# Scans over both halves of a state, and four of sixteen products with B moved to ScalarE

## The reference

```python
u, z = split(x @ Win.T)                       # 2 x 256 channels
u = silu(causal_conv4(u) + convb)
dtr, B, C = split(u @ Wx.T)                   # 8, 16 and 16 columns
dt = softplus(dtr @ Wdt.T + bdt)              # 256 channels
A = -exp(Alog)                                # 256 x 16
def step(h, ins):                             # over 512 positions; h is 256 x 16
    h = exp(dt_t[..., None] * A) * h + (dt_t * u_t)[..., None] * B_t[:, None, :]
    y_t = einsum('bdn,bn->bd', h, C_t)
y = (ys + u * D) * silu(z)
out = y @ Wout.T
# x + forward(xn) + flip(backward(flip(xn))), with layer norms around it
```

## Time and profile before

| | |
|---|---|
| time, three runs | 2227.23, 2219.51, 2219.79 us (median 2219.79) |
| the profiled execution | 2225.48 us, of which the span of the profile is 2223.7 |
| granted clock of TensorE, mean over the span | 0.82 |
| busy: VectorE, TensorE, GpSimd, ScalarE | 73%, 73%, 55%, 53% |
| the changed phase | from 0 to about 1050 us |

### The profile page before, as it was taken

How to read it: one execution, slowest core, us unless ns; L and a number is a source line. 1 busy time by engine, 2 the same in 40 slices (tenths; PEclk the granted TensorE clock), 3 DMA queues, 4 the chain that set the end, 5 groups by cost and what they waited for, 6 DMA issues and landing times.

```text
span 2223.7 us, 29267 instructions
## 1 busy us (share of the span) xinstructions
PE 1614.2 (73%) x7664; PEld 938.7 (42%) x7664; DVE 1626.8 (73%) x2538; ACT 1174.6 (53%) x1906; POOL 1233.7 (55%) x1097
## 2 busy tenths in 40 slices
PE   3677676766677666765376887877879888897888
PEld 1445454544455444544133343443434434343443
DVE  3999999999999999996262738456384654837455
ACT  4565555656565555561146391754727357282751
POOL 2777677777777677774336280643717346181541
PEclk8888777877888777775567598898989989899999
DMA  4212022121212011120301000000100001000000
GB/s 149 82 77 84 21 82 81 76 95 76 95 76 91 21 74 81 76 91 12 115 6 36 11 27 11 16 35 16 36 8 9 34 16 36 16 10 26 11 0 15
DMA packets 39620, 107.23 MB, mean 48 GB/s; under 512 B 4128, under 2 KB 30048, under 8 KB 34368
## 3 DMA queue, kind: packets, MB, share of 16 engines
q1 hardware_dynamic: 39520, 106.24, 12.6%
HBM read 92.99 MB, written 8.65 MB: 46 GB/s over the span
## 4 chain that ended last, share of the span: by engine, by line
issue 25%; POOL 13%; PE 6%; DVE 4%; DMA 2%; ACT 1%; SPq 0%; POOLq 0%; DVEq 0%; ACTq 0%
POOL pp L1892 9%; DMA k<-k_scratch 1%; DVE mx L1583 1%; PE pbk L1224 1%; PE po L1231 1%; PE pa L1218 1%; PE og L1167 1%; PE scores L1119 1%; PE scores L1117 1%; POOL ln_r L1822 0%; DVE rec L1611 0%; POOL kp L1855 0%; ACT pt L1414 0%; POOL rotk L1851 0%; PE scores L1147 0%
## 5 line engine op out<-in xcount | busy, mean ns | idle before, releaser
L731 POOL TENSOR_TENSOR hc<-hb,cb 128x512 f32<-128x512 f32 x512 | 653.8, 1295 | 249.3 <-DVE hb L610 221.4
L610 DVE TENSOR_TENSOR_SCAN hb<-da,dbu 128x512 f32<-128x512 f32 x512 | 599.5, 1202 | 5.6 <-DVE stats L635 4.0
L499 ACT ACTIVATE da<-dt,a_neg 128x512 f32<-128x512 f32 x512 | 351.9, 717 | 352.9 <-DVE hb L610 303.9
L331 PE MATMUL yp<-ident,hc 128*128 128x128 f32 x2048 | 359.0, 317 | 65.0 <-POOL hc L731 64.6
L1892 POOL TENSOR_TENSOR pp<-pt,pp 128x512 f16<-128x512 f32 x320 | 365.0, 1151 | 71.7 <-ACT pt L1414 71.3
L331 PEld LDWEIGHTS yp<-ident,hc 128*128 128x128 f32 x2048 | 297.9, 166 | 174.3 <-POOL hc L731 93.2
L603 DVE TENSOR_TENSOR dbu<-dtu,bp 128x512 f32<-128x512 f32 x512 | 323.8, 677 | 4.0 <-PE bp L319 3.2
L1583 DVE TENSOR_REDUCE mx<-scores 128x1 f32<-128x384 f32 (+3 forms) x352 | 218.4, 636 | 131.0 <-PE scores L1119 127.9
L1693 DVE SCALAR_TENSOR_TENSOR ga<-th,pa 128x512 f32<-128x512 f32 x128 | 87.6, 685 | 246.4 <-ACT th L1429 246.4
L1413 ACT ACTIVATE pp<-scores,lift 128x512 f16<-128x512 f32 x320 | 221.5, 692 | 46.3 <-PE scores L1147 45.4
L319 PE MATMUL bp<-st,sel 96*128 96x512 bf16 x256 | 116.4, 455 | 151.7 <-DVE dbu L603 149.0
(11 more groups left out here) (181 smaller groups left out, 2265.6 us busy)
## 6 DMA issues: line engine op xcount, KB each, us to landing
cb<-c_scratch SPq DMA_DIRECT2D x16, 3072.0 KB, 11.8
cb<-c_scratch SPq DMA_DIRECT2D x16, 1024.0 KB, 4.6
q<-q_scratch SPq DMA_DIRECT2D x24, 288.0 KB
q_scratch<-qp SPq DMA_DIRECT2D x24, 128.0 KB
q<-q_scratch SPq DMA_DIRECT2D x24, 96.0 KB
xin<-in_x SPq DMA_DIRECT2D x8, 256.0 KB, 11.5
xres<-xin SPq DMA_DIRECT2D x8, 256.0 KB, 2.4
xres<-xln SPq DMA_DIRECT2D x8, 256.0 KB, 2.6
```

What stands on the lines that cost most here:

```text
L331: last = nc.tensor.matmul(yp[:, c, h * P:(h + 1) * P], src[:, c * P:(c + 1) * P], ident[:, :], is_transpose=True, start=(s < 0 and h == 0 ...
L499: nc.scalar.activation(da[:, s % NDA, :], dt[:, d, h, :], ACT.Exp, scale=a_neg[:, d, h, n:n + 1]).then_inc(da_done, 1)
L610: nc.vector.tensor_tensor_scan(hb[:, s % NHB, :], da[:, s % NDA, :], dbu[:, s % 2, :], 0.0, ALU.mult, ALU.add).then_inc(scan_done, 1)
L731: nc.gpsimd.tensor_tensor(hc[:, s % NHC, :], hb[:, s % NHB, :], cb[:, d, s // 2, :], ALU.mult).then_inc(hc_done, 1)
```

## The change

- `hb`, `da`, `dbu` and `hc` hold a whole state: both halves, 1024 columns. There is one scan a state instead of two. The first column of each half of `da` is 0, so that the scan starts anew at the half; ScalarE writes the other 511.
- The store of decays is eight states instead of eight steps (the same eight slots, each twice as wide); `hc` has two slots of a state instead of eight of a step.
- For twelve states TensorE writes B's broadcast, once for each half, into `dbu` itself (`pe_fill`), and VectorE multiplies in place with one instruction of 1024 columns. For states 4, 7, 10 and 13 VectorE doesn't multiply. There, `dtu` is transposed once a unit (`pe_dtut`, `act_dtut`), so that time lies on the partitions and B's values are a scalar for each partition (`bt`, from 16 short passes, `pe_bt`, and a copy). ScalarE multiplies (`act_dbut`, four instructions of 256 columns a state), and TensorE transposes the result back into `dbu` (eight passes). The scan then reads `dbu` directly.
- `pe_fill` of state n waits for scan n-2, since that frees the slot of `dbu`.
- `ud` goes; u * D is now a product of u with a diagonal matrix `diag_d` (16 passes, in `pe_y` with n = -1).
- A scan stands directly behind its own product.
- The front moves to later steps: on TensorE two steps (four for d = 0) for u, z in one piece at step 22, xd and `bt` at 23, dt at 25 and 26; on ScalarE all of silu, xd and softplus stand behind the unit's last decay. dt and dtu stand together behind scan 14. `pe_dt` also waits for `bt`. The output product goes in two pairs, at steps 13 and 14; `dve_end` stands behind scans 9, 10, 11 and 13.
- `cb` is one buffer for both directions, loaded in four groups of four states (1 MB each), each when its states of the unit before are used. SP's order becomes: C of direction 0, C of direction 1 but its last group, store, `xres`, x of the batch after next, last group. x is thus loaded behind the store of the batch before last.

```diff
+BY_ACT = (4, 7, 10, 13)
+BY_DVE = tuple(n for n in range(NS) if n not in BY_ACT)
+NA, ND = len(BY_ACT), len(BY_DVE)
+NGROUP = 4
+PER_GROUP = NS // NGROUP
+LAG_N = 2
...
-        ud = sb("ud", [P, NH2, SEQ])
-        cb = sb("cb", [P, NDIR, NS, SEQ])
+        diag_d = sb("diag_d", [P, NDIR, NH2, P])
+        dtut = sb("dtut", [P, NDIR, TC, DI])
+        bt = sb("bt", [P, NDIR, TC, NS])
...
-        NDA, NHB, NHC = 8, 4, 8
-        da = sb("da", [P, NDA, SEQ])
...
-        hb = sb("hb", [P, NHB, SEQ])
-        hc = sb("hc", [P, NHC, SEQ])
-        bp = pb("bp", [P, 2, SEQ])
-        dbu = pb("dbu", [P, 2, SEQ])
+        NDA, NHB, NHC, NTB = 8, 4, 2, 2
+        da = sb("da", [P, NDA, NH2, SEQ])
+        hb = sb("hb", [P, NHB, NH2 * SEQ])
+        hc = sb("hc", [P, NHC, NH2, SEQ])
...
+        dbut = sb("dbut", [P, NTB, TC, DI])
+        dbu = pb("dbu", [P, 2, NH2, SEQ])
         yp = pb("yp", [P, TC, DI])
         wp = pb("wp", [P, 2, SEQ])
...
+        def sp_batch(sp, b, last=False):
+            sp_c_write(sp, b + 1, 0)
+            for g in range(NGROUP):
+                sp_c_load(sp, b + 1, 0, g)
+            sp_c_write(sp, b + 1, 1)
+            for g in range(NGROUP - 1):
+                sp_c_load(sp, b + 1, 1, g)
+            sp_store(sp, b)
+            sp_keep(sp, b + 1)
+            if not last:
+                sp_x_load(sp, b + 2)
+            sp_c_load(sp, b + 1, 1, NGROUP - 1)
...
                 pe.wait_ge(xd_done, count(xd_done, b, 4 * d + 2))
+                pe.wait_ge(bt_done, count(bt_done, b, d + 1))
...
+        def pe_fill(pe, b, d, n):
+            pe.wait_ge(scan_done, count(scan_done, b, NS * d + n - 1))
+            if n in BY_DVE:
+                if n == 0:
+                    pe.wait_ge(part_done, count(part_done, b, d + 1))
+                    pe.wait_ge(xd_done, count(xd_done, b, 4 * d + 3))
+                for h in range(NH2):
+                    last = nc.tensor.matmul(dbu[:, n % 2, h, :], sel[:, n, :], st[:, d, :], start=True, stop=True)
+            else:
+                pe.wait_ge(dbut_done, count(dbut_done, b, NA * d + BY_ACT.index(n) + 1))
+                for h in range(NH2):
+                    for c in range(TC):
+                        last = nc.tensor.transpose(dbu[:, n % 2, h, c * P:(c + 1) * P],
+                                                   dbut[:, BY_ACT.index(n) % NTB, c, h * P:(h + 1) * P], ident[:, :])
+            last.then_inc(b_ready, 1)
+        def pe_bt(pe, b, d):
+            pe.wait_ge(silu_done, count(silu_done, b, 4 * d + 4))
+            for c in range(TC):
+                for h in range(NH2):
+                    last = nc.tensor.matmul(wp[:, 1 - d, c * NS:(c + 1) * NS], u[:, h, c * P:(c + 1) * P],
+                                            wx[:, d, h, 0:NS], start=(h == 0), stop=(h == 1))
+            last.then_inc(bt_ready, 1)
...
+        def pe_y(pe, b, d, n):
+            if n < 0:
+                pe.wait_ge(diag_set, NDIR * NH2)
                 pe.wait_ge(yg_done, count(yg_done, b, d))
...
+                for h in range(NH2):
+                    for c in range(TC):
+                        last = nc.tensor.matmul(yp[:, c, h * P:(h + 1) * P], u[:, h, c * P:(c + 1) * P],
+                                                diag_d[:, d, h, :], start=(h == 0 and c % 2 == 0), stop=False,
+                                                skip_group_check=True)
...
             last.then_inc(y_added, 1)
...
+        def pe_front(pe, b, d, s):
+            if s == 13 and d == 0:
+                pe_xt(pe, b)
+            for i in range(NH2 * NTAP):
+                if s == (14, 15, 15, 16, 17, 18, 18, 19)[i] + 2 * (d == 0):
+                    pe_u(pe, b, d, i)
+            if s == 22:
+                pe_z(pe, b, d, 0)
+                pe_z(pe, b, d, 1)
+            if s == 23:
+                pe_xd(pe, b, d)
+                pe_bt(pe, b, d)
+            if s in (25, 26):
+                pe_dt(pe, b, d, s - 25)
         def pe_unit(pe, b, d, front=None, tail=None, after=None):
...
             for s in range(STEPS):
...
+                n = s // 2
+                if s % 2 == 0:
+                    if n + 1 < NS:
+                        pe_fill(pe, b, d, n + 1)
+                    elif after:
+                        pe_fill(pe, *after, 0)
+                else:
+                    if n < LAG_N and tail:
+                        pe_y(pe, *tail, NS - LAG_N + n)
+                    if n == LAG_N + 1:
+                        for m in range(-1, n - LAG_N):
+                            pe_y(pe, b, d, m)
+                    if n > LAG_N:
+                        pe_y(pe, b, d, n - LAG_N)
+                if s == 1:
+                    pe_dtut(pe, b, d)
+                if tail and s == 8:
                     pe_ygt(pe, *tail)
...
+                if tail and tail[1] == 1 and s in (13, 14):
+                    pe_out(pe, tail[0], 2 * (s - 13))
+                    pe_out(pe, tail[0], 2 * (s - 13) + 1)
                 if front:
...
+                    pe_front(pe, *front, s)
             if not after:
...
+                for n in range(NS - LAG_N, NS):
+                    pe_y(pe, b, d, n)
         @block.tensor
         def _(pe):
...
+        def act_dbut(act, b, d, n):
+            k = BY_ACT.index(n)
+            if k == 0:
+                act.wait_ge(dtut_done, count(dtut_done, b, d + 1))
+            slot_before = BY_ACT[k - NTB] + (NS * d if k >= NTB else NS * (d - 1))
+            act.wait_ge(b_ready, count(b_ready, b, slot_before + 1))
+            for c in range(TC):
+                last = nc.scalar.activation(dbut[:, k % NTB, c, :], dtut[:, d, c, :], ACT.Copy,
+                                            scale=bt[:, d, c, n:n + 1])
+            last.then_inc(dbut_done, 1)
         def act_da(act, b, d, s):
             n, h = s // 2, s % 2
             if s == 0:
                 act.wait_ge(dt_done, count(dt_done, b, 2 * d + 1))
...
+            if h == 0:
+                act.wait_ge(scan_done, count(scan_done, b, NS * d + n + 1 - NDA))
+            nc.scalar.activation(da[:, n % NDA, h, 1:], dt[:, d, h, 1:], ACT.Exp,
                                  scale=a_neg[:, d, h, n:n + 1]).then_inc(da_done, 1)
...
+        def act_front(act, b, d, at):
+            if at == 25 and d == 0:
                 act_xpad(act, b, 0)
...
                 act_xpad(act, b, 1)
...
+            if at == 31:
                 act_silu_u(act, b, d, 0)
                 act_silu_u(act, b, d, 1)
                 act_silu_z(act, b, d, 0)
                 act_silu_z(act, b, d, 1)
                 act.preload_act_table_set("natural_log_exp_and_others")
...
+                act_xd(act, b, d, 0)
+                act_xd(act, b, d, 1)
+                act_bt(act, b, d)
+                act_xd(act, b, d, 2)
+                act_xd(act, b, d, 3)
                 for h in range(NH2):
                     for k in range(4):
                         act_soft(act, b, d, h, k)
...
         def act_unit(act, b, d, front=None, tail=None):
             for s in range(STEPS):
                 act_da(act, b, d, s)
...
+                if s == 5:
+                    act_dtut(act, b, d)
+                if s % 2 == 1 and s // 2 + 1 in BY_ACT:
+                    act_dbut(act, b, d, s // 2 + 1)
+                if tail and s in (22, 23):
+                    act_ygt(act, *tail, s - 22)
                 if front:
                     act_front(act, *front, s)
...
+        def dve_dbu(dve, b, d, n):
+            if n == 0:
                 dve.wait_ge(dt_done, count(dt_done, b, 2 * d + 2))
...
+            dve.wait_ge(b_ready, count(b_ready, b, NS * d + n + 1))
+            nc.vector.tensor_tensor(dbu[:, n % 2], dtu[:, d], dbu[:, n % 2], ALU.mult).then_inc(dbu_done, 1)
+        def dve_scan(dve, b, d, n):
+            if n in BY_DVE:
+                dve.wait_ge(dbu_done, count(dbu_done, b, ND * d + BY_DVE.index(n) + 1))
+            else:
                 dve.wait_ge(b_ready, count(b_ready, b, NS * d + n + 1))
...
+            dve.wait_ge(da_done, count(da_done, b, STEPS * d + 2 * n + 2))
+            dve.wait_ge(hc_done, count(hc_done, b, NS * d + n + 1 - NHB))
+            nc.vector.tensor_tensor_scan(hb[:, n % NHB, :], da[:, n % NDA].rearrange("p h t -> p (h t)"),
+                                         dbu[:, n % 2].rearrange("p h t -> p (h t)"), 0.0,
                                          ALU.mult, ALU.add).then_inc(scan_done, 1)
...
+            for n in range(NS):
+                if n in BY_DVE:
+                    dve_dbu(dve, b, d, n)
+                if front and front[1] == 0 and n == 1:
                     dve_ln_stats_wait(dve, front[0])
...
+                if tail and tail[1] == 1 and n == 11:
                     dve.wait_ge(end_step, count(end_step, tail[0], 4))
...
+                dve_scan(dve, b, d, n)
+                if tail and n == LAG_N:
                     dve_yg(dve, *tail)
...
```

(23 more changed lines are left out.)

221 lines of the change are left out of this document (75 added, 146 removed).

## The result

The changed kernel takes 2310.78 us, the median of four runs (2296.15 to 2328.43), against 2219.65 for the kernel before (2219.37 to 2227.23): a ratio of 1.0405 with a 95% interval of 1.0326 to 1.0484. That is 4% slower, where 0.4% was forecast; 2229 was named and 2188 to 2265 given. The profiled execution is the slowest of the four, 2328.43 us with a span of 2326.3.

What follows compares the result with a forecast made beforehand. VectorE was taken to bound the state-space phase. Savings of 77.5 us against 72 of stalls, 12 for the clock and 3 at the ends gave +9.5: 2235 profiled, 2229 for the median, range 2188 to 2265.

Steps and rivals of the forecast that it cites:

- The sum on VectorE: VectorE's state-space work: wider scans and fewer products bring a unit's states from 54.6 to 50.0 us, 77.5 saved in all.
- Rival 2: A scan behind its own product waits for nothing: 29 us in all, about 17 after stalls, giving 2212; chance 0.07.
- TensorE, where the gain goes: TensorE's front work, bunched between fills, makes VectorE wait: 72 us of stalls, plus 12 for slower clock.
- 12 for the clock: TensorE's granted clock drops after waits in or before the front: 0.85 us in each of 14 units.
- Unit A: Unit that prepares a direction 0: VectorE waits 3.2 us at state 13 and 0.95 before dt, together 4.2.
- Unit B: Unit that prepares a direction 1 and finishes a batch: VectorE waits 1.4, 2.1, 0.9 and 1.2 us, together 5.6.
- rival 1: The cover holds: TensorE's front fits between fills without stalls, giving 2145 us, or 2181 with half the stalls; chance 0.2.
- rival 4: The x load, issued later by SP, arrives 7 us late in 7 units, 50 us more, giving 2278; chance 0.08.
- rival 3: TensorE's taps in unit A start at a slow clock: 28 to 56 us more, 2257 to 2285; chance 0.17.
- ScalarE, GpSimd, DMA: None bounds: ScalarE gains 6.5 us a unit, GpSimd's products stay at 2.49 a state, C's loads are hidden.
- The direction: That the whole kernel comes out slower than 2231 us, given 0.42 against 0.28 for faster and 0.30 for between.
- three signs of being wrong: VectorE idle under 20 us in the phase; bt far from 1.9 us; dbu or scans waiting for GpSimd or decays.

Runs made afterwards that it cites:

- e4: The changed kernel with each scan waiting for its decay and hc slot first and its product last: 2292.4 us, 1.0297 of the kernel before.

## Why the prediction was wrong

**The step that failed is "The sum on VectorE".** It said 77.5 us saved if nothing else ever waits. Two parts of it are false.

- *The operations between SBUF and SBUF were left at the durations of the kernel before.* They cost 73.8 us more. Neither the sum nor a rival had it. It could have been read: the earlier trace rows show dt with 1.54 and dtu with 1.19 for the same number of columns with both inputs in SBUF; the 0.35 between them was the lock. That such operations wait for GpSimd is shown by the kernel that measures them alone and by dt in PSUM. How much it would grow could not be read. The trace after shows that xn, x1t and dtu meet a busy GpSimd more often, and dt, x1t and xn with more of its work ahead; why GpSimd runs in such stretches is argued from its queue, and who goes first is open.
- *A state with a product costs 3.44.* The bare pattern does, and e4 shows it in the kernel: 1.24 to the scan, 2.20 behind it. The code has three waits there, and a pair takes 3.62. With 2.21 for a state without a product, a unit's states take 52.3 instead of 50.0: 36 us in 16. Rival 2 (the own wait is free) is wrong, and the sentence of the Trainium skill's "VectorE: DVE Perf Modes", the section on the DRAIN, doesn't hold here: the wait costs 0.11 to 0.13 us with one semaphore (1.24 against 1.13 in the kernel of its own and 1.11 in the earlier trace rows) and 0.3 with three.

**"TensorE, where the gain goes" held in its sum.** 72 for stalls and 12 for the clock stood against 73.4 us of waits for fills and 5.6 of dt for t_ln. Unit A: 3.2 before scan 13 and 0.95 before dt; measured 2.45 and 0.70. Unit B: 5.6 without the clock; 1.97, 2.84, 1.78 and 0.82 measured, 7.4, with the wait for res at 2.65 where 2.6 was named. B^T took 1.85 for 1.9. So the cover did not hold (rival 1), and the x load landed 2.8 us from its issue (rival 4). The slow clock in A's taps (rival 3) didn't come: the granted clock was 1.00 from 558 to 582. In B, behind the wait for res, it was 0.79 for 2.2 us and 0.59 for 3.0, by my estimate 1.7 us of work lost, which is about what B's waits are above the 5.6 without the clock. **"ScalarE, GpSimd, DMA"** was right that they don't bound and wrong to stop there: GpSimd doesn't bound and yet sets the length of other instructions.

The sum again by what was measured: the forecast of 2235 for a profiled execution, plus 74 for the port, plus 36 for the states, less 5 for the waits, is 2340, against 2328. Of the 12 between, 5 are the other phase, which came out shorter (1184.4 against 1189.4); the rest isn't divided. The direction had the largest chance, 0.42, but for stalls and clock alone, which leave +9.5 of the 103 measured, so that it came out is in part luck. None of the three signs of being wrong that it named looks at the length of an instruction, and none appeared, but for 6.6 us of a scan's wait that are booked to decays and hc; the upper bound of 2265 didn't hold the port.

## What to carry to other kernels

Before you change what runs between VectorE and GpSimd, list the instructions on VectorE that have all their operands in SBUF, and look whether one form has several durations in the trace; if the long ones begin beside a busy GpSimd, that spread is the lock. Here such instructions came to take twice their time while GpSimd's busy time stayed the same, so GpSimd's busy share doesn't foretell it. Leave one operand in PSUM, or give the instruction to ScalarE. Put the wait that is met last behind the others, and price moved TensorE work at the clock of the place that it moves to. Compare the phase that was changed before you compare totals: here an untouched phase moved by up to 43 us from kernel to kernel.

## What the runs showed of the hardware

- Beside back-to-back 512-column products on GpSimd, a 128-column scale and shift from SBUF to SBUF went from 0.27 to 1.23 us and a 1024-column sum of two SBUF inputs from 1.16 to 2.14; forms with an operand in PSUM kept 0.33 and 1.16, scans 2.21.
- Reading and writing the columns backwards changes nothing: 9.74 us for eight beside GpSimd, 9.81 forwards, 2.14 each way alone.
- The order of waits that are all met in the end is worth 0.17 us an instruction (1.41 to 1.24).
- The same 1024-column sum took 1.20 us with GpSimd idle and 3.67 on average with 2.59 us of its stretch left; with 0.31 us of a product left it took 1.40 in one kernel and 3.85 in another.
- Sixteen matmuls with 16 moving columns take 1.85 us at the full clock, 0.116 each, and 3.43 behind a wait of 5.16, at a granted clock of 0.50.
